# One step list for the first three turns and one for the last two, with the clip masks released in two halves

## What is computed

```python
x = layernorm(x + L0(x, adj))      # q,k,v; softmax(q k^T/8 + bias) v; Wf
# L1, per head a:
h = x @ W[a]; th = tanh(h)
attn = leaky_relu(th @ w_src[a] + (th @ w_dst[a]).T, 0.2)
attn = softmax(where(adj, attn, -999)); f = elu(attn @ h + b)
gate = sigmoid(x @ H_w.T + H_b)
x = layernorm(x + gate * f + (1 - gate) * x)
```

## Time and profile before

| | us |
|---|---|
| median of 3 runs | 1114.17 (1114.08 to 1117.92) |
| profiled execution, its own time | 1116.9 |
| its span | 1114.9 |
| PE busy in the span | 1052.9 |
| DVE busy | 914.5 |
| POOL busy | 684.7 |
| ACT busy | 655.8 |

### The profile page before, as it was taken

How to read it: one execution, slowest core, us unless ns; L and a number is a source line. 1 busy time by engine, 2 the same in 40 slices (tenths; PEclk the granted TensorE clock), 3 DMA queues, 4 the chain that set the end, 5 groups by cost and what they waited for, 6 DMA issues and landing times.

```text
span 1114.9 us, 28421 instructions
## 1 busy us (share of the span) xinstructions
PE 1052.9 (94%) x9199; PEld 898.5 (81%) x9199; DVE 914.5 (82%) x2289; ACT 655.8 (59%) x2060; POOL 684.7 (61%) x605
## 2 busy tenths in 40 slices
PE   5999999999999999999999999999999999999775
PEld 4788888888888888888888888888888888888653
DVE  1669889798897979889797988979798897988866
ACT  3847466574746757475574746657574665747432
POOL 0347566575666667567576756666575675766664
PEclk9999999999999999999999999999999999999995
DMA  7110010101001010010101001010100101000000
GB/s 187 32 31 1 30 33 9 52 0 43 16 28 31 7 52 0 28 31 14 45 7 52 0 28 31 7 52 0 58 0 28 31 7 52 0 28 2 29 1 29
DMA packets 34722, 31.00 MB, mean 28 GB/s; under 512 B 15872, under 2 KB 34688, under 8 KB 34688
## 3 DMA queue, kind: packets, MB, share of 16 engines
q1 hardware_dynamic: 34688, 30.57, 9.0%
HBM read 17.98 MB, written 12.58 MB: 27 GB/s over the span
## 4 chain that ended last, share of the span: by engine, by line
PE 74%; DVE 13%; issue 7%; ACT 3%; POOL 2%; SPq 1%; DMA 1%; DVEq 0%; ACTq 0%; POOLq 0%
PE p_bank L477 46%; PE t_bank L616 4%; DVE weights L934 4%; PE scores L539 4%; PE context L560 3%; PE context L630 3%; PE t_bank L548 3%; PE context L636 3%; PE t_bank L644 2%; PE t_bank L586 2%; PE t_bank L607 1%; ACT probs0T L721 1%; DVE xT L814 1%; PE t_bank L509 1%; DVE cT L814 1%
## 5 line engine op out<-in xcount | busy, mean ns | idle before, releaser
L1041 POOL TENSOR_TENSOR w_rows<-qwT,own_head 96x1536 fp32r<-96x1536 f32 x64 | 176.0, 2752 | 78.9 <-ACT qwT L777 78.8
L934 DVE SCALAR_TENSOR_TENSOR weights<-t_bank,pqw,clip 128x128 f32<-128x128 f32 x768 | 207.8, 342 | 14.1 <-PE t_bank L616 11.7
L1034 POOL TENSOR_TENSOR prod<-th,w_sd 128x768 f32<-128x768 f32 x64 | 117.3, 1832 | 130.9 <-ACT th L740 130.9
L712 ACT ACTIVATE probs<-masked,neg_max 128x128 f32<-128x128 f32 x384 | 148.7, 392 | 2.8 <-DVE neg_max L852 2.5
L477 PE MATMUL p_bank<-w_h,x1T 128*128 128x384 f32 x576 | 114.3, 343 | 9.5 <-DVE x1T L814 9.5
L1046 POOL TENSOR_TENSOR f_b<-f_raw,bias 128x384 f32<-128x384 f32 x64 | 68.4, 1068 | 85.3 <-DVE f_raw L949 85.3
L477 PE MATMUL p_bank<-w_v,xT 128*128 128x384 f32 x576 | 116.5, 346 | 0.8
L477 PE MATMUL p_bank<-w_g,x1T 128*128 128x384 f32 x576 | 115.7, 346 | 0.0
L477 PEld LDWEIGHTS p_bank<-w_h,x1T 128*128 128x128 f32 x576 | 102.0, 190 | 16.6 <-DVE x1T L814 13.3
L477 PE MATMUL p_bank<-w_f,cT 128*128 128x384 f32 x576 | 114.3, 342 | 0.8 <-DVE cT L814 0.6
L899 DVE TENSOR_TENSOR gate_sum<-p_bank,gate_bias 128x384 f32<-128x384 f32 x64 | 34.9, 546 | 95.7 <-PE p_bank L477 95.7
(11 more groups left out here) (107 smaller groups left out, 2329.8 us busy)
## 6 DMA issues: line engine op xcount, KB each, us to landing
x_in<-in_x_dram SPq DMA_DIRECT2D x16, 768.0 KB, 4.7
out_dram<-y_out SPq DMA_DIRECT2D x64, 192.0 KB, 1.9
adj_in<-in_adj_dram SPq DMA_DIRECT2D x16, 64.0 KB, 4.3
probs0T<-in_L_gnn_Wq_dram SPq DMA_DIRECT2D x1, 576.0 KB, 5.7
weights<-in_L_gnn_Wk_dram SPq DMA_DIRECT2D x1, 576.0 KB, 6.8
x_res<-in_L_gnn_Wv_dram SPq DMA_DIRECT2D x1, 576.0 KB, 7.3
probs<-in_L_gnn_Wf_dram SPq DMA_DIRECT2D x1, 576.0 KB, 7.7
x<-in_L_gnn_W_dram SPq DMA_DIRECT2D x3, 192.0 KB, 6.3
```

Source lines behind the costliest of these rows:

```text
L712: last = act.activation(probs0[:, k % 2, b, j * P:(j + 1) * P], masked[:, k % 2, b * PAIRS + j, :], ACT.Exp, bias=neg_max[:, b * PAIRS + j ...
L934: last = dve.scalar_tensor_tensor(out=weights[:, g % 2, n, :], in0=src[:, i * P:(i + 1) * P], scalar=pqw[:, g % 2, 0, n:n + 1], in1=clip[: ...
L1034: pool.tensor_tensor(prod[:], over_heads(th[:], 2), w_sd[:], ALU.mult).then_inc(s_prod, 1)
L1041: pool.tensor_tensor(w_rows[0:QW_ROWS, k % 2], over_heads(qwT[:, k % 2, 1, :].bitcast(F32), H1), per_head(own_head[:], P), ALU.mult).then_ ...
```

## The change

`load`, `first` and `second` become one list per engine, `PE_BEGIN` and its like, and `drain` and `last` become `PE_END` and its like. A step now carries its turn as a third number, so that steps of different turns can stand mixed. The function `bank` looks up the step two uses back with its turn. Between `begin` and the loop, PE waits once until the last two uses of each kind of bank are read. The steps in all lists are the same in number; in the loop's lists some have changed places. The clip mask of graphs 2k and 2k + 1 may be overwritten as soon as the weights of graphs up to 2k + 1 are clipped, where it had to wait for all four; and each `e` of a new graph waits for the mask that it reads.

```diff
 PE_LOOP = [
-    ("v", 0), ("x1T", 0), ("qk", 0), ("qk", 1), ("x1T", 1), ("qk", 2), ("h", 0), ("gate", 0), ...
+    ("v", 0), ("x1T", 0), ("x1T", 1), ("qk", 0), ("qk", 1), ("qk", 2), ("h", 0), ("gate", 0), ...
...
+PE_BEGIN = [
+    ("xT", 0, -2), ("xT", 1, -2), ("xT", 2, -2), ("xT", 3, -2), ("qk", 0, -1), ("qk", 1, -1), ("qk", 2, -1),
+    ("qk", 3, -1), ("qk", 4, -1), ("qk", 5, -1), ("v", 0, -1), ("s", 0, -1), ("ob", 0, -1), ("s", 1, -1),
...
 POOL_LOOP = [
-    ("prod", 0), ("x_res", 0), ("prod", 1), ("rows", 0), ("rows", 1), ("prod", 2), ("norm", 0), ("fb", 0),
+    ("prod", 0), ("prod", 1), ("rows", 0), ("rows", 1), ("x_res", 0), ("norm", 0), ("prod", 2), ("fb", 0),
...
-def phases(eng, step, engine, NG):
-    for name, k in ORDERS["load"][engine]:
-        step(name, k, -2, "load")
-    for name, k in ORDERS["first"][engine]:
-        step(name, k, -1, "first")
-    for name, k in ORDERS["loop"][engine]:
-        step(name, k, 0, "second")
+def phases(eng, step, engine, NG, between=None):
+    for name, k, d in ORDERS["begin"][engine]:
+        step(name, k, d, ("begin", d))
+    if between:
+        between()
     with eng.Fori(1, NG - 2) as u:
-        for name, k in ORDERS["loop"][engine]:
-            step(name, k, u, "loop")
-    for name, k in ORDERS["drain"][engine]:
-        step(name, k, NG - 2, "drain")
-    for name, k in ORDERS["last"][engine]:
-        step(name, k, NG - 1, "last")
+        for name, k, d in ORDERS["loop"][engine]:
+            step(name, k, u, ("loop", d))
+    for name, k, d in ORDERS["end"][engine]:
+        step(name, k, NG - 2 + d, ("end", d))
...
+            def banks_free():
+                for freed in (t_freed, p_freed):
+                    for before, kb, db in bank_uses(freed, "begin")[-2:]:
+                        s, per = freed[before]
+                        te.wait_ge(s, upto(db + SHIFT.get(before, 0), per, kb + 1))
...
                 elif name == "clip":
-                    wait(dve, s_e, upto(g1, THIRDS * GROUP, THIRDS * GROUP))
+                    wait(dve, s_e, upto(g1, THIRDS * GROUP, THIRDS * 2 * (k + 1)))
...
                 elif name == "e":
+                    if r == 0:
+                        dve.wait_ge(s_mx, upto(g1, 2, g // 2 + 1))
```

More of the change, by code:

```diff
@@ L39 @@
[L39 to L43, removed]
@@ L52 @@
-    ("mixa", 0), ("qwlo", 2), ("wlog", 3), ("mixb", 0), ("rden1", 1), ("sum1", 0), ("qwlo", 3), ("clo", 0),
[4 rows of a table removed]
[L57 to L60, removed]
+    ("mask", 1), ("e", 3), ("rden0", 0), ("max", 1), ("e", 4), ("e", 5), ("rden1", 0), ("f_raw", 0), ("x1lo", 3),
@@ L117 @@
-POOL_LAST = [
-    ("prod", 0), ("prod", 1), ("rows", 0), ("prod", 2), ("rows", 1), ("fb", 0), ("rows", 2), ("prod", 3), ("ex", 0),
-    ("rows", 3), ("fb", 1), ("rstd1", 0), ("ex", 1), ("fb", 2), ("ex", 2), ("fb", 3), ("rstd1", 1), ("ex", 3),
-    ("rstd1", 2), ("rstd1", 3),
-]
-ORDERS = {
-    "load": {"PE": [("xT", g) for g in range(GROUP)],
-             "ACT": [("whi", 0)] + [("xhi", g) for g in range(GROUP)] + [("whi", 1)],
-             "DVE": [("wlo", 0)] + [("xlo", g) for g in range(GROUP)] + [("wlo", 1)],
-             "POOL": []},
-    "first": {"PE": PE_FIRST, "ACT": ACT_FIRST, "DVE": DVE_FIRST, "POOL": POOL_FIRST},
-    "loop": {"PE": PE_LOOP, "ACT": ACT_LOOP, "DVE": DVE_LOOP, "POOL": POOL_LOOP},
-    "last": {"PE": PE_LAST, "ACT": ACT_LAST, "DVE": DVE_LAST, "POOL": POOL_LAST},
-}
@@ L131 @@
-ORDERS["second"] = ORDERS["loop"]
-ORDERS["drain"] = {e: [(n, k) for n, k in steps if n not in ("xT", "xhi", "xlo")] for e, steps in ORDERS["loop"].items()}
-BEFORE = {"first": "load", "second": "first", "loop": "second", "drain": "loop", "last": "drain"}
+    ("rstd0", 0), ("rstd1", 0), ("fb", 2), ("ex", 2), ("rstd0", 1), ("fb", 3), ("rstd1", 1), ("rstd0", 2), ("ex", 3),
+    ("rstd1", 2), ("rstd0", 3), ("rstd1", 3),
+]
+POOL_BEGIN = [
+    ("x_res", 0, -1), ("norm", 0, -1), ("norm", 1, -1), ("norm", 2, -1), ("rstd0", 0, -1), ("norm", 3, -1),
+    ("rstd0", 1, -1), ("rstd0", 2, -1), ("prod", 0, 0), ("rows", 0, 0), ("rstd0", 3, -1), ("prod", 1, 0),
+    ("rows", 1, 0), ("x_res", 0, 0), ("fb", 0, 0), ("prod", 2, 0), ("ex", 0, 0), ("norm", 0, 0), ("prod", 3, 0),
+    ("norm", 1, 0), ("rows", 2, 0), ("norm", 2, 0), ("rows", 3, 0), ("fb", 1, 0), ("norm", 3, 0), ("ex", 1, 0),
+    ("rstd1", 0, 0), ("rstd0", 0, 0), ("fb", 2, 0), ("ex", 2, 0), ("rstd0", 1, 0), ("fb", 3, 0), ("rstd1", 1, 0),
+    ("ex", 3, 0), ("rstd0", 2, 0), ("rstd0", 3, 0), ("rstd1", 2, 0), ("rstd1", 3, 0),
+]
@@ L134 @@
+ENGINES = ("PE", "ACT", "DVE", "POOL")
+ORDERS = {
+    "begin": dict(zip(ENGINES, (PE_BEGIN, ACT_BEGIN, DVE_BEGIN, POOL_BEGIN))),
+    "loop": {e: [(name, k, 0) for name, k in steps]
+             for e, steps in zip(ENGINES, (PE_LOOP, ACT_LOOP, DVE_LOOP, POOL_LOOP))},
+    "end": dict(zip(ENGINES, (PE_END, ACT_END, DVE_END, POOL_END))),
+}
 WEIGHTS = ("q", "k", "v", "f", "h")
@@ L511, in step @@
                 elif name == "qk":
-                    if phase == "first" and k == 0:
+                    if turn == FIRST and k == 0:
                         te.wait_ge(s_wlo, 2)
@@ L588, in step @@
                 elif name == "h":
-                    if phase == "second" and k == 0:
+                    if turn == SECOND and k == 0:
                         te.wait_ge(s_wlo, 5)
@@ L645, in step @@
                     last.then_inc(pe["sumsT"], 1)
[L647 removed]
+            phases(te, step, "PE", NG, banks_free)
         @block.scalar
```

243 lines of the change are left out of this document (148 added, 95 removed), and 72 rows, old and new, of tables (DVE_BEGIN, DVE_END, DVE_LOOP, PE_BEGIN).

## The result

The changed kernel takes 1120.15 us (median of 14 runs, 1119.42 to 1121.15), the kernel before 1113.61 (14 runs). The ratio is 1.0051, with a 95% interval of 1.0042 to 1.0061. I had forecast 1100 and faster; it is slower by just over half a per cent.

The account below looks back on a forecast made before the run. PE was taken to bound the middle, with DVE also full at turn ends and the last turn a chain of waits. Gains of 1.5 + 3.3 + 9.4 = 14.2 us off 1114.17 gave 1100.0; range 1090 to 1110, 8 in 10.

Parts of the forecast that it names:

- The beginning: First projection to end of turn 0: mixing fills PE's 3.5 us of idle time, 1.5 us gained after deductions.
- the wait at the boundary: Between `begin` and the loop: PE may not start `v` before DVE has read the last `f`, costing 0.7 us.
- the mixture: Beginning: mixed steps fill PE's 3.5 us of idle time, with 1 us left for new waits.
- The loop: 13 turns: fewer PE waits gain 0.25 us a turn, 3.3 in all; bounds nothing to 14 us.
- ends near 253.9 again: Loop, turn's end: DVE's `f_raw` 3 ends as late as before, with one `clip` more and 0.2 us less idle ahead.
- the relaxed wait of `clip` and the added one of `e` cost nothing: DVE's mask waits: free, since the mask is written well ahead of the weights that read it.
- at about half a us for a full row: Loop, turn's end: eleven DVE steps from `f_raw` 3 to `gsum` 3 need 4.8 us, so `v` starts about 258.9.
- the rule on contention: End: two-SBUF-input or two-port DVE operations and GpSimd exclude each other; could make the end some 4 us later.
- whatever PE gained earlier in the turn is handed back here: Loop: PE's first `xT` waits for DVE's `f_raw` 3, so earlier gains in the turn are lost there.
- `x_res` at nothing: Loop: moving `x_res` behind `rows` 1 on POOL neither gains nor costs, as weights keep their usual pace beside `rows`.
- the slower rival: Loop: `x_res` holds DVE where it is needed, up to 3.50 us a turn, giving 1132 us; chance 0.06.
- The end: Last turns: mixing group 15's layer 1 into its layer 0 fills the chain's waits, 9.4 us gained.

Follow-up runs that it names:

- e4: All old orders written as the new code's three lists, against the kernel before: 1123.87 us, ratio 1.0096, turn 66.34 us.
- e5: e4 with the wait of `e` for `clip` taken out: 1117.74 us, ratio to before 1.0013, turn 66.03 us.
- e6: The kernel after with only the wait of `e` for `clip` taken out: 1115.24 us, ratio to before 1.0008, turn 66.66 us.
- e7: e6 with `x1` 1 three steps earlier in DVE's loop, away from GpSimd's `ex` 3: 1108.22 us, ratio to before 0.9945, turn 66.24 us.
- e15: e7 with PE's `wb` 4 put back ahead of `pv1` 0: 1108.85 us, ratio to before 0.9937, turn 66.07 us.
- e11: e7 with PE's `wb` 4 and `f` 2 put back in their old places: 1111.40 us, ratio to before 0.9973, turn 66.33 us.
- e13: e8 with `x_res` moved behind `rows` 1 on GpSimd: 1107.16 us, ratio to before 0.9919, turn 66.01 us.
- e3: e4 with the new order of the end; first turns and loop stay old: 1116.09 us, ratio to before 1.0016.
- e8: The kernel after with the old loop order on all engines and no wait of `e` for `clip`: 1106.67 us, ratio to before 0.9922.
- e14: e8 with DVE's wait for `clip` kept, once a turn in the loop at `x1lo` 0: 1106.90 us, ratio to before 0.9917.

## Why the prediction was wrong

**The beginning** came out right, 1.5 us forecast and 1.55 measured, but its terms did not, so there is luck in it. I had PE start 0.3 us later than the 14.28 of the earlier trace rows; it starts its first `qk` at 13.38, 0.9 earlier:

```profile
13.38 4.21 PE L574 MATMUL p_bank<-xT,w_q 128*128 128x512 f32 x9 [4.29 <-DVE w_k L918]
```

Against that the wait at the boundary took 1.1 us where I had put 0.7, and of the idle time behind the start the mixture won 1.55 - 0.9 + 1.1 = 1.75 us where I had 2.5.

**The loop** was wrong in sign: 3.3 us gained was forecast, 11.9 lost measured. Its range had no loss in it at all ("nothing" was its lower bound, because DVE would end each turn as late as before). Two steps of the working failed, and with them that DVE "ends near 253.9 again": `f_raw` 3 starts 60.25 us behind `v` 0 in the kernel before (253.43 less 193.18) and 61.56 behind it in the kernel after (253.19 less 191.63).

The first is "the relaxed wait of `clip` and the added one of `e` cost nothing". I had asked whether the mask is ready, which it is, and not what the wait adds to the handover from PE to DVE. It costs 0.31 us a turn in the old order (e4 to e5) and 0.33 in the new one (after to e6), 4 us in 13 turns.

The second is that I took every DVE operation at its usual duration in its new place ("at about half a us for a full row"). I did have the rule on contention, and priced it for the end only, where by the earlier trace rows an `out` was held; in the loop I weighed it for `x_res` alone. The same holding decides at the turn's end, where DVE is full: `x1` beside `ex` costs 0.42 us a turn in the new order (e6 to e7).

A smaller loss that I hadn't priced: `pv1` 0 ahead of `wb` 4 takes 0.17 (e7 to e15). These three make 0.33 + 0.42 + 0.17 = 0.92 of the 0.96 us a turn. What remains, 0.04, is the best that was tried of the new order (e15, 66.07), so the 0.25 us a turn that I had forecast as its gain was found in none of these kernels: the removed `pT` wait comes back at `qwT`. That "whatever PE gained earlier in the turn is handed back here" came true in its outcome, but not by the mechanism that it named. `xT` does not wait for `f_raw` in the kernel after; that wait appears only in e11.

`x_res` at nothing was right (e13; in the kernel after it starts at 219.03, near the 220 that were forecast, and `sda` takes 0.18), and with it the slower rival's mechanism was wrong. It was right that GpSimd holds DVE where DVE is needed, but it is `ex` and not `x_res`, for 0.76 us and not 3.5, and it is one of three losses.

**The end** gained 7.0 us between the two profiles where I had forecast 9.4. Its terms held where they were counted. DVE's work behind the first scores was to be 81.0 us; it is 52.27 + 28.83 = 81.1. The last `x1` was to come at 1067 on the old time scale; it comes at 1077.11 - 10.31 = 1066.8. Layer 1 of the last group begins on PE at 1055.13, which is 1044.8 there, where I had 1046. What was too small is the idle time of DVE: it was to be 2.6 + 4.0 + 6 = 12.6; it is 4.9 + 10.0 = 14.9, and these 2.3 us are the missing 2.4. Since the last `x1` came on time, they show behind it. There I had 34 us to the last `out`, where my own sum (1103.2 less 1067) makes it 36, and the trace has 38.3, with PE at a granted clock of 0.76.

By medians the end gained less. In both profiled executions the turns of the loop had a granted clock of 1.00 and even lengths, so I put the 3.3 us by which that of before lies above its median, and the 0.1 by which that of after lies below, to the end. Then it gained 7.0 - 3.4 = 3.6 us, an estimate. I had subtracted from the median a gain that was read in an execution above it. In e4 and e5 the old end takes 127.2 and 127.4 us in place of 129.66. In the same form of the code the new end alone brings 7.8 us by medians (e4 to e3), with e4's wide spread in it, and 6.4 between the two ends of the table.

With loop and wait as before, beginning and end bring 1114.13 to 1106.67 us (e8), 0.9922 with 0.9893 to 0.9950. So the most that the change brought in the orders that were tried is about 0.8%, 7.5 us in e8 and 8.3 in e14 against the before of its series, and not 14. The safe form of it, with the wait for `clip` kept and put at `x1lo`, is e14: 1106.90 us, and with e8 and e13 the fastest measured. The three don't differ by more than their intervals.

One thing stays open. The end takes 119.7 to 124.2 us in kernels with the same new lists for it. The granted clock of its last stretches differs too (in the last 15 us 0.76 in e7 at 119.7, 0.61 in e8 at 123.95). Much of this is no property of the kernels: e8 alone took 1104.59 us at a granted clock of 0.992 over the span and 1109.44 at 0.987, and the latter was profiled. Corrected by how far each profiled execution lies from its kernel's median, the ends take 120.5 to 122.8 us. Whether the clock is cause or effect there no run separates.
